# A selective-scan layer and a Hadamard feed-forward on one core: every fourth dt broadcast made by DMA, and some loads moved

## The reference, cut to what matters

```
x = x + L0_attn(layernorm(x))      # RMS norm, selective scan, gate; then RMS norm and a gated MLP of 704
x = x + L0_ffn(layernorm(x))       # silu(x W1) * (x W3), Walsh-Hadamard over 1024, times W2

# inside L0_attn
z, x, B, C, dt_raw = split(u @ in_proj_w.T)
dt = softplus(dt_raw @ dt_proj_w.T + dt_proj_b)            # 256 channels
h  = exp(dt * A) * h + (dt * x) * B                        # state: 256 channels x 32
y  = sum over the 32 states of h * C
```

## Time and profile before

| | us |
|---|---|
| median of 3 runs | 1182.16 (1180.35 to 1183.41) |
| the profiled execution | 1184.15 |
| its span, first to last instruction | 1182.3 |
| busy: TensorE matmuls | 1060.2 |
| busy: VectorE | 1020.8 |
| busy: GpSimd | 918.8 |
| busy: ScalarE | 602.5 |

### The profile page before, as it was taken

How to read it: one execution, slowest core, us unless ns; L and a number is a source line. 1 busy time by engine, 2 the same in 40 slices (tenths; PEclk the granted TensorE clock), 3 DMA queues, 4 the chain that set the end, 5 groups by cost and what they waited for, 6 DMA issues and landing times.

```text
span 1182.3 us, 13029 instructions
## 1 busy us (share of the span) xinstructions
PE 1060.2 (90%) x3848; PEld 537.0 (45%) x3848; DVE 1020.8 (86%) x1161; ACT 602.5 (51%) x1118; POOL 918.8 (78%) x532
## 2 busy tenths in 40 slices
PE   3576689899998999999999999899999989997978
PEld 1221134446453554545454554446453644445535
DVE  4589899999999999999999999999999999995322
ACT  3455565546655565546655565546655554443120
POOL 1589999878998899878998899878998889785000
PEclk9687689999999999999999999999999999899989
DMA  5998988867668586766667586766676676630000
GB/s 171 216 208 193 232 210 205 179 144 171 165 146 176 119 202 142 164 151 167 161 154 167 120 201 143 165 156 161 161 165 140 141 175 145 137 77 18 1 1 18
DMA packets 99925, 176.38 MB, mean 149 GB/s; under 512 B 13008, under 2 KB 21648, under 8 KB 99600
## 3 DMA queue, kind: packets, MB, share of 16 engines
q1 hardware_dynamic: 97984, 171.32, 63.5%
q0 software_dynamic: 1152, 4.19, 1.0%
q10 hardware_dynamic: 720, 0.04, 0.0%
HBM read 150.34 MB, written 8.39 MB: 134 GB/s over the span
## 4 chain that ended last, share of the span: by engine, by line
PE 60%; issue 11%; DVE 10%; POOL 9%; ACT 6%; DMA 1%; SPq 1%; ACTq 0%; DVEq 0%; POOLq 0%
PE p_r L478 17%; PE p_r L467 13%; PE p_r L473 8%; PE p_y L433 7%; PE p_dt L422 7%; POOL h_s L1026 6%; DVE h_s L817 5%; PE p_r L484 4%; DVE bt_s L800 2%; ACT p_dt L574 2%; POOL bt_s L1002 2%; PE p_r L453 2%; ACT tok L591 1%; PE p_r L457 1%; ACT tok L589 1%
## 5 line engine op out<-in xcount | busy, mean ns | idle before, releaser
L1026 POOL TENSOR_TENSOR h_s<-h_s,c_s 128x1024 f32<-128x1024 f32 x256 | 604.2, 2363 | 94.1 <-DVE h_s L817 77.8
L574 ACT ACTIVATE p_dt<-p_dt,an_s 128x512 f32<-128x512 f32 x512 | 332.3, 659 | 328.3 <-PE p_dt L422 328.2
L422 PE MATMUL p_dt<-kdt,pick_s 128*128 128x512 f32 x512 | 324.5, 659 | 57.4 <-DVE h_s L817 46.2
L817 DVE TENSOR_TENSOR_SCAN h_s<-p_dt,carry,bt_s 128x512 f32<-128x512 f32 x256 | 321.1, 1272 | 7.8 <-ACT p_dt L574 6.1
L817 DVE TENSOR_TENSOR_SCAN h_s<-p_dt,bt_s 128x512 f32<-128x512 f32 x256 | 305.2, 1211 | 25.0 <-ACT p_dt L574 19.2
L478 PE MATMUL p_r<-nT,w_s 128*128 128x512 f32 x512 | 244.0, 605 | 3.1 <-ACT nT L735 3.1
L1002 POOL TENSOR_TENSOR bt_s<-bt_s,b_s 128x1024 f32<-128x1024 f32 x96 | 227.0, 2365 | 9.3 <-DMA xr_s<-xb_s 4.9
L800 DVE TENSOR_TENSOR bt_s<-bt_s,p_b 128x1024 f32<-128x1024 f32 x160 | 192.4, 1202 | 6.7 <-DMA bt_s<-dx_rows 6.7
L422 PEld LDWEIGHTS p_dt<-kdt,pick_s 128*128 128x128 f32 x512 | 99.0, 199 | 206.8 <-DVE h_s L817 115.8
L467 PE MATMUL p_r<-nT,gu_s 128*128 128x512 f32 x352 | 169.0, 604 | 3.3 <-ACT nT L729 3.2
L433 PE MATMUL p_y<-h_s,ysel_s 128*32 128x512 f32 x1024 | 145.8, 643 | 15.0 <-POOL h_s L1026 14.9
(11 more groups left out here) (81 smaller groups left out, 729.2 us busy)
## 6 DMA issues: line engine op xcount, KB each, us to landing
bt_s<-dx_rows SPq DMA_DIRECT2D x512, 256.0 KB, 5.3
kdt<-st_dt SPq DMA_DIRECT2D x64, 128.0 KB, 5.7
tok<-in_x SPq DMA_DIRECT2D x8, 512.0 KB, 7.2
xr_s<-xb_s SPq DMA_DIRECT2D x64, 64.0 KB, 4.4
b_s<-xb_s SPq DMA_DIRECT2D x64, 64.0 KB, 4.9
dx_rows<-dx_s SPq DMA_DIRECT2D x16, 256.0 KB, 4.9
xo<-in_x SPq DMA_DIRECT2D x8, 512.0 KB, 7.1
out<-res POOLq DMA_DIRECT2D x8, 512.0 KB, 5.8
```

The source lines that it names most:

```text
L422: nc.tensor.matmul(p_dt[DT_BANK[u]][:, :], sel, kdt[:, h, p // 16, :], start=True, stop=True)\
L574: A(p_dt[DT_BANK[u]][:, :], p_dt[DT_BANK[u]][:, :], ACT.Exp, scale=an_s[:, c:c + 1]).then_inc(a_dA, 1)
L817: V.tensor_tensor_scan(h_s[:, u % 8, :], p_dt[DT_BANK[u]][:, :], bt_s[:, u % 16, :], carry[:, u:u + 1] if par else 0.0, ALU.mult, ALU.add) ...
L1026: G.tensor_tensor(h_s[:, two, :], h_s[:, two, :], c_s[:, h, :].unsqueeze(1).broadcast_to([P, 2, T]), ALU.mult)\
```

## The change

It has six parts.

- From tile 1 on, units 3, 7, 11, ... 63 (`ROW_UNITS`) have no spread matmul. `keep_rows` also stores the block dt_s to a second DRAM buffer dt_rows, and `load_row_pair` reads the rows of two such units at a time, broadcast to 32 partitions, into dtr4_s (four slots of [128, 512] in SBUF). It is issued at slots u = 2, 10, 18, ... of SyncE's walk, for the pair of units 8q+3 and 8q+7 with q = u/8 + 1. The decay of such a unit reads dtr4_s, waits itself for scan u-3 (u-2 for unit 63), and writes the same p_dt bank as before.
- `keep_dt` waits for the row store before it overwrites dt_s.
- In the start, `load_b(0, 1)` is issued before the first row store instead of after the second run.
- out_s is loaded at slot 48 of body 0 instead of 44. The first half of the gate weights is loaded at slot 60 of body 0 instead of 48, the second at slot 1 of body 1 instead of slot 56 of body 0. down_s follows at slot 6 of body 1 instead of 2.
- TensorE waits for the input weights before its first transpose, not at the first stage that uses them. ACT waits for its scale parameters where they are first used, not before its first instruction on the moments.
- Before the w2 transform TensorE waits for the last users of its three banks as PLAN names them.

```
+ROW_UNITS = range(3, U, 4)
+def by_row(i, u):
+    return i >= 1 and u in ROW_UNITS
+def spreads(i, u):
+    return u + 1 if i == 0 else U + (i - 1) * (U - len(ROW_UNITS)) + u + 1 - made(ROW_UNITS, u)
+        dtr4_s = sb("dtr4_s", [P, 4, T])
...
+            def load_row_pair(t, par, q):
+                sp.wait_ge(l_dt_rows, ((t - 1) * 2 + q // 4 + 1) * 16)
+                sp.wait_ge(a_dA, t * U + 8 * q - 8)
+                for g in range(GH):
+                    rows_of_g = dt_rows[par, q // 4].rearrange("(a b g) t -> g a b t", a=4, g=GH)[g, 3]
+                    src = rows_of_g[2 * (q % 4):2 * (q % 4) + 2]
+                    sp.dma_start(dtr4_s[NS * g:NS * g + NS, 2 * (q % 2):2 * (q % 2) + 2, :],
+                                 src.partition_broadcast(NS)).then_inc(l_row4[q % 2], 16)
             def keep_rows(t, par, h):
+                if t >= 1:
+                    sp.wait_ge(a_dt, t * 2 + h + 1)
+                    sp.dma_start(dt_rows[par, h], dt_s[:, :]).then_inc(l_dt_rows, 16)
                 sp.wait_ge(g_dx, t * 2 + h + 1)
                 sp.dma_start(dx_rows[par, h], dx_s[:, :]).then_inc(l_rows, 16)
...
                 load_b(0, 0)
+                load_b(0, 1)
                 keep_rows(0, 0, 0)
                 load_run(0, 0, 0)
                 load_dt(0, 0)
                 load_run(0, 0, 1)
                 load_xr(0, 0, 1)
-                load_b(0, 1)
                 load_run(0, 0, 2)
...
-                if i == 0 and u == 44:
+                if i == 0 and u == 48:
                     sp.dma_start(out_s[:, :, :], out_w).then_inc(l_w["out"], 16)
-                if i == 0 and u in (48, 56):
-                    k = (u - 48) // 8
-                    sp.dma_start(gu_s[:, k, :, :], gu_w[:, k, :, :]).then_inc(l_w["gu"], 16)
-                if i == 1 and u == 2:
+                if (i, u) in ((0, 60), (1, 1)):
+                    sp.dma_start(gu_s[:, i, :, :], gu_w[:, i, :, :]).then_inc(l_w["gu"], 16)
+                if i == 1 and u == 6:
...
+                    if u % 8 == 2:
+                        q = u // 8 + 1
+                        if (units and i >= 1 if q < 8 else units and pre):
+                            load_row_pair(i + q // 8, par if q < 8 else 1 - par, q % 8)
...
-                    if (units if u + 2 < U else pre):
+                    if not by_row(i + (u + 2) // U, (u + 2) % U) and (units if u + 2 < U else pre):
                         spread(i + (u + 2) // U, (u + 2) % U)
...
-                act.wait_ge(pe_dt, i * U + u + 1)
                 c = UH * (u // UH) + unit_channel(u)
-                A(p_dt[DT_BANK[u]][:, :], p_dt[DT_BANK[u]][:, :], ACT.Exp, scale=an_s[:, c:c + 1]).then_inc(a_dA, 1)
+                if by_row(i, u):
+                    q = u // 8
+                    act.wait_ge(l_row4[q % 2], ((i - 1) * 4 + q // 2 + 1) * 64)
+                    act.wait_ge(v_sc, i * U + u - DT_GAP[u] + 1)
+                    dt_in = dtr4_s[:, u // 4 % 4, :]
+                else:
+                    act.wait_ge(pe_dt, spreads(i, u))
+                    dt_in = p_dt[DT_BANK[u]][:, :]
+                A(p_dt[DT_BANK[u]][:, :], dt_in, ACT.Exp, scale=an_s[:, c:c + 1]).then_inc(a_dA, 1)
...
                 if h or from_tile(t, 1):
                     act.wait_ge(g_dx, m)
+                    if m > 2:
+                        act.wait_ge(l_dt_rows, (m - 2) * 16)
```

More of the change, by code:

```diff
@@ L167, in build @@
         l_xrep = [sem(f"l_xrep{h}") for h in range(2)]
-        l_rows = sem("l_rows")
+        l_rows, l_dt_rows = sem("l_rows"), sem("l_dt_rows")
+        l_row4 = [sem(f"l_row4{k}") for k in range(2)]
         l_dx = [sem(f"l_dx{k}") for k in range(4)]
@@ L197, in build @@
         dx_rows = nc.dram_tensor("dx_rows", [2, 2, P, T], F32).ap()
+        dt_rows = nc.dram_tensor("dt_rows", [2, 2, P, T], F32).ap()
         x_t = x.rearrange("b s d -> (b s) d")
@@ L271, in load_dt @@
             def load_dt(t, h):
-                made_dt, spread_dt = number(t * 2 + h + 1), number((t - 1) * U + UH * (h + 1))
+                made_dt, spread_dt = number(t * 2 + h + 1), spreads(t - 1, UH * (h + 1) - 1) if t else 0
                 sp.wait_ge(a_dth, made_dt)
@@ L492, in transform_w2 @@
                     pe.wait_ge(w_had, 6)
-                    for stage, n, t in (("uT", 1, 1), ("xb", 0, 1), ("dtr", 0, 1), ("z", 1, 0), ("c1", 0, 0)):
-                        done(stage, n, t)
+                    for r in range(RING):
+                        stage, n = [p for p in PLAN[r::RING] if p[0] in PRE | MID and p[4] < W2_SLOT][-1][:2]
+                        done(stage, n, tile_of(stage, 0))
                 if k >= RING:
@@ L521, in body @@
                         weights_there(i, u)
-                    if known(i) and i == -1 and u == ENDS["xb", 0]:
-                        pe.wait_ge(l_w["in"], 16)
                     if known(i) and i == -1 and u == ENDS["dtp0", 0]:
@@ L538, in _ @@
             pe.wait_ge(l_w["ident"], 16)
+            pe.wait_ge(l_w["in"], 16)
             bodies(pe, body)
@@ L555, in _ @@
             act.wait_ge(w_an, 2)
-            act.wait_ge(l_w["par"], 64)
             def keep_w2(k):
@@ L662, in body @@
                             if u == ENDS["uT", k] + 1:
+                                if i == -1:
+                                    act.wait_ge(l_w["par"], 64)
                                 act.wait_ge(mm["uT"], nt * 2 + k + 1)
```

## The result

The changed kernel takes 1176.45 us (median of 10 runs, 1171.39 to 1179.39) against 1181.83 (10 runs beside them): a ratio of 0.9940, 95% interval 0.9926 to 0.9954. It is faster by 0.6%, and the forecast was 1163: less than a third of the gain came. The profiled execution took 1176.25 (span 1174.3), 7.9 us less than the one of before; the medians differ by 5.4, because the profiled execution of before lies 2.3 above its median.

A forecast was written before the change was run, and what follows sets the result against it. It took TensorE and a nearly full VectorE to bound the kernel in turns. Start -2.0, relief net -19 (26 less 7) and tile 1 +1.5 gave -19.5 us, a median of 1163; own range 1154 to 1171, 8 in 10 1149 to 1178.

The forecast's parts named there:

- Those four: VectorE's waits for a decay (15.0 us), the w2 result (9.0), the down result (6.8) and a tanh (5.1).
- w2 result: VectorE's six waits for w2 at the tile seams, 9.0 us; fewer spreads, unit 63's above all, would save 7.0.
- Decays: VectorE's 27 waits for decays, 15.0 us; 3.8 saved directly and 5.5 through an earlier TensorE, together 9.
- Down result: VectorE's seven waits for the down stage, 6.8 us; the spreads of units 19 to 31 would save 5.
- Tanh and the rest: VectorE's remaining 13.4 us of waits; half of the 10 that name TensorE or ScalarE would go, 5 us.
- Taken back by GpSimd: GpSimd, nearly full in a tile's third eighth, would take back 1 us in each of seven tiles.
- Clock: Rival, 10%: an emptier TensorE near unit 35 falls to 1.2 GHz in five spared tiles, 1.1 us each: 1169.
- Start: Earlier input work and B's second half before the first row store bring the first scan 2.0 us earlier.
- Tile 1: Added row pairs and gate weights back up the transfers there and cost 1.5 us, bounds 0 and 7.
- Steady transfers: Added row transfers in the steady tiles cost 0, with queue 1 at 83% instead of 68%.
- the first rival: Little is converted: VectorE and GpSimd are the bound, only the w2 gap and a little remain, 1177; chance 20%.

The follow-up runs named there:

- exp_dt: The changed kernel with Exp in place of Softplus where dt is made, so no table loads in a tile; 1167.00 us, ratio 0.9882.
- half_nodma: The changed kernel with every odd unit a row unit (32 instead of 16), their dt a constant 0.01 and no row transfers; 1168.21 us, ratio 0.9871.
- unit63: The changed kernel with unit 63 as its only row unit and one row pair loaded per tile; 1178.16 us, ratio 0.9963.
- no_root: The changed kernel with GpSimd's square root of the second norm replaced by a product of constants; 1170.73 us, ratio 0.9904.
- order_before: The kernel before with only ScalarE's decay of unit 11 moved one slot earlier, ahead of the normalisation; 1179.40 us, ratio 0.9977.
- loads_only: The changed kernel with all row transfers made but every spread matmul kept and every decay reading PSUM; 1183.98 us, ratio 1.0004.
- start_only: The kernel before with only the start's part of the change, all spreads kept and weights at their old slots; 1181.87 us, ratio 0.9991.

## Why the prediction was wrong

**Where its reading failed.** "Those four are four fifths, and each of them is TensorE being late." The wait list names the last releaser; for the decays, the largest of the four, the prediction did not look at what that releaser had been doing. The decays of units 56 and 57, 7.0 of the 15.0 us, are late behind two table loads in ScalarE's own queue: exp_dt takes these waits to 0, twice the relief of TensorE (half_nodma) only to 4.9. The decay of unit 11 stands behind a normalisation that waits for GpSimd. Of the 9 us forecast for the decays 3.1 came, 2.3 of them at unit 63, and 3.8 were added at unit 11.

**Term by term.**
- w2 result: forecast 7.0, its wait fell by 6.1. Near, and by the mechanism that was told: unit63 alone takes 6.5 us off the seams. The seams are 9.2 shorter in all, with 2.3 of the decay of unit 63 and 0.8 that no wait of the list shows.
- Decays: forecast 9, came 3.1 (2.3 at unit 63, 0.8 at units 55 to 58).
- Down result: forecast 5, came 0 beside the tanh. The term let TensorE's lead add up over units 19 to 31, since TensorE had no idle time there; now it pauses just before the down stage (0.35 us in tile 4). The 0.47 us of tile 4 that are left are the ones that VectorE takes at the tanh of unit 26: one lead was counted in two terms.
- Tanh and the rest: forecast 5, came 2.9 at unit 26 and 0.4 at units 20 to 22. The waits for w3's result and for a tanh at units 38 to 40 rose; they are in the clock's term.
- Taken back by GpSimd: forecast 7, came 4.0, in the place next to the one named: units 10 to 15, not the third eighth. no_root shows that it is GpSimd's work. Sign and mechanism were right.
- Clock: forecast 0 in the sum, came 4.1. As a rival it had five falls at 1.1 us, and 10%. Only four tiles had been spared, since tile 7 had a fall before too; these four give 4.0. The mechanism of that rival was at work beside the failed terms. The Trainium skill (TensorE: Matmul & The Clock Gate, Part 1) says that the clock is throttled by default and released by activity. The fall of tile 4 fits that, with 1.62 us busy of 4.00 ahead of it. The two rows that the prediction set beside the rule don't show it: tile 6, which kept its clock, was the emptier of the two (3.1 us idle against 2.6).
- Start: forecast 2.0, came 2.07 in this pair of profiles. The mechanism is right; the size is partly chance, since later profiles have the first scan at 38.04 to 39.55 with the new start and at 40.43 with the old one (order_before).
- Tile 1: forecast 1.5, came 0 to nearly 4 by execution (GpSimd's wait for a run 0.53 and 5.13). That it varies was not foreseen.
- Steady transfers at 0: right by the steady tiles of loads_only, and ScalarE waits for no row pair in the steady tiles. Queue 1 is at 86.4% where 83% was forecast: 25.17 MB in 0.864 x 131.28 = 113.4 us is 4.5 us for a MB, against 4.4.

With the terms that came, 13.3 us were converted and not 26, and 4.0 + 4.1 returned: the first rival (little is converted, 1177) is the one that describes the run, with the clock in addition. Its reason was GpSimd at 98%. That was a part of the truth; the order of ScalarE's queue and TensorE's pause before the down stage were the others.

## What to carry to other kernels

Follow a wait one engine further than the list names it, and split its sum by place: if the releaser's own queue is full just before (table loads, a normalisation that waits in turn), relief anywhere else is worth little there. Let a lead add up only as far as the relieved engine's next wait for another engine. Price a relief by the places where the relieved engine is the last to come, and expect each gain to be met one stage on by the next full engine; here one spread of sixteen earned most of what was earned. Count the stretches at 1.2 GHz before and after, and set them apart from the rest: here they took 4.1 us of a gain of 13.3.

## What the runs showed of the hardware

- A root of 128x4 elements takes GpSimd 1.03 us, a product of the same size 0.19.
- A table load takes ScalarE 1.28 us, and a single softplus among exponentials costs two, 2.56 us in front of the next decay, for 0.66 us of work.
- Executions of the same kernel differ in the number of stretches at 1.2 GHz and in a run's landing in tile 1. The kernel after spreads over 8.0 us in ten runs; the kernel before over 3.2 in the ten beside them, but over 8.6 in the 28 beside start_only.
- A stretch of 3.4 us at 1.2 GHz near unit 35 makes units 38 to 42 of a tile 8.3 to 9.5 us long instead of 7.9 to 8.2.
- With 32 broadcast pieces of 128 KB and two stores more in a tile (4.8 MB), queue 1 takes 4.5 us for a MB instead of 4.4.
